# Which engine normalises the tokens of the third and fourth group in a Mamba-2 scan

## The reference, cut to what matters

```python
x = x + mamba2(_layernorm(x))          # the phase of this case
x = x + cross_attention(_layernorm(x), ctx, mask)
x = x + mixture_of_experts(_layernorm(x))

def _layernorm(x, axis=-1, eps=1e-05):
    m = jnp.mean(x, axis=axis, keepdims=True)
    v = jnp.var(x, axis=axis, keepdims=True)
    return (x - m) / jnp.sqrt(v + eps)

# mamba2, HID 256, 64 heads of 64 channels, state 128:
proj = hidden_states @ W_in.T          # z, xBC, dt
xBC = silu(conv4(xBC) + conv_b)        # x, B, C
dt = softplus(dt + dt_bias)
y = (C B^T * decay) @ (x * dt) + D_param * x      # over a sequence of 256
g = y * silu(z)
out = rmsnorm(g) * norm_w @ W_out.T
```

## Time and profile before

| | |
|---|---|
| median of three runs | 1668.36 us (1668.01 to 1669.1) |
| the profiled execution | 1666.68 us, of which the span from first to last instruction is 1664.9 us |
| mean granted TensorE clock | 0.989 of full speed |
| TensorE busy (matmul) | 1592.1 us, 96% |
| VectorE busy | 1250.4 us, 75% |
| ScalarE busy | 1198.9 us, 72% |
| GpSimd busy | 834.6 us, 50% |
| the 128 steps of the scan | from about 43 us to about 920 us |

### The profile page before, as it was taken

One profiled execution on the slowest core, in us unless ns is written; L12 is line 12 of the kernel. 1 busy time (PEld: TensorE's weight loads), 2 busy tenths in 40 slices (PEclk: granted clock), 3 DMA queues, 4 the chain that ended last, 5 costly groups with the idle time before them and its releaser, 6 DMA issues. The chain is left out here.

```text
span 1664.9 us, 29161 instructions
## 1 busy us (share of the span) xinstructions
PE 1592.1 (96%) x9876; PEld 1280.0 (77%) x9876; DVE 1250.4 (75%) x1954; ACT 1198.9 (72%) x2504; POOL 834.6 (50%) x677
## 2 busy tenths in 40 slices
PE   4998999999999999999999999999969999999999
PEld 3776777777777777777777667877748889999888
DVE  6899999999898999998899656766566534433355
ACT  5998899999999999999999566766624334444331
POOL 5798786565555555555565422211124563335460
PEclk8999999999999999999999999999979999999999
DMA  7555454444444454464542100000214323222231
GB/s 287 184 171 178 172 188 169 138 162 157 156 158 147 152 166 166 154 247 157 169 156 89 57 1 14 14 14 27 104 73 166 127 105 111 93 93 93 78 101 51
DMA packets 76238, 209.84 MB, mean 126 GB/s; under 512 B 9152, under 2 KB 32960, under 8 KB 74304
## 3 DMA queue, kind: packets, MB, share of 16 engines
q1 hardware_dynamic: 70432, 181.90, 32.0%
q0 software_dynamic: 5664, 26.09, 4.5%
HBM read 170.99 MB, written 36.96 MB: 125 GB/s over the span
## 5 line engine op out<-in xcount | busy, mean ns | idle before, releaser
L1011 PE MATMUL banks<-pair_hi,m_wxz 128*128 128x512 f32 x1024 | 352.3, 405 | 3.9 <-DVE pair_lo L664 2.3
L739 DVE SCALAR_TENSOR_TENSOR m_xc<-banks,m_cw,m_xc 128x510 f32<-128x510 f32 (+2 forms) x384 | 285.4, 743 | 11.0 <-ACT m_xc L502 1.3
L385 POOL TENSOR_TENSOR m_mat<-m_mat,m_cb_off 128x512 f32<-128x512 f32 x128 | 166.3, 1300 | 205.8 <-DVE m_mat L751 197.6
L516 ACT ACTIVATE m_mat<-m_a_all,m_cum 128x256 f32<-128x256 f32 x512 | 258.9, 506 | 1.6 <-PE m_ps_y L1052 1.6
L1068 PE MATMUL m_ps_out<-m_won,m_gT 128*128 128x256 f32 x1024 | 242.9, 380 | 4.7 <-POOL m_gT L394 3.2
L1011 PEld LDWEIGHTS banks<-pair_hi,m_wxz 128*128 128x128 f32 x1024 | 193.9, 189 | 42.8 <-issue 2.7
L394 POOL TENSOR_TENSOR m_gT<-m_gy,m_zs 128x512 f32<-128x512 f32 x128 | 167.0, 1305 | 107.2 <-DVE m_gy L781 106.9
L1068 PEld LDWEIGHTS m_ps_out<-m_won,m_gT 128*128 128x128 f32 x1024 | 191.4, 189 | 36.7 <-POOL m_gT L394 6.6
L519 ACT ACTIVATE m_mat<-m_a_all,m_cum 128x128 f32<-128x128 f32 x512 | 203.4, 397 | 0.0
L1011 PE MATMUL banks<-pair_lo,m_wxz 128*128 128x512 f32 x512 | 201.0, 393 | 0.0
L1052 PE MATMUL m_ps_y<-m_mat,m_xdt 128*64 128x256 f32 (+1 forms) x2048 | 194.7, 332 | 0.0
(11 more groups left out here) (348 smaller groups left out, 3400.4 us busy)
## 6 DMA issues: line engine op xcount, KB each, us to landing
m_a_all<-a_by_head SPq DMA_DIRECT2D x128, 512.0 KB, 4.0
m_wxz<-w_split SPq DMA_DIRECT2D x96, 512.0 KB, 5.0
w_split<-m_wxz SPq DMA_DIRECT2D x32, 512.0 KB, 3.0
raw<-in_w_gate_up POOLq DMA_DIRECT2D x9, 1280.0 KB, 6.8
raw<-in_w_xz SPq DMA_DIRECT2D x32, 256.0 KB, 3.9
raw<-in_w_down POOLq DMA_DIRECT2D x9, 640.0 KB, 7.8
x_sorted<-f_gT_hi SPq DMA_DIRECT2D x1, 4992.0 KB, 16.4
f_xg<-x_sorted SPq DMA_DIRECT2D x39, 128.0 KB, 2.6
```

The lines of the kernel that those rows point to most:

```text
L385: pool.tensor_tensor(off, off, cb_off[:, g * BG:(g + 1) * BG, :].rearrange("p b t -> p (b t)").unsqueeze(1) .broadcast_to([P, HPT, BG * P] ...
L516: act.activation(first_rows(u, h, b), a_all[u][:, h, b * SEQ:(b + 1) * SEQ].rearrange("p (j t) -> p j t", t=P), ACT.Relu, bias=cum[:, t, h ...
L739: dve.scalar_tensor_tensor(out=out[:, :, k:], in0=ps[:, :, 0:SEQ - k], scalar=cw[:, c, TAPS - 1 - k:TAPS - k], in1=out[:, :, k:], op0=ALU. ...
L1011: last = pe.matmul(ps[:, :], w, a, start=m == 0, stop=m == len(terms) - 1)
```

## The change

The eight normalisations of the tiles of the third and fourth group move from GpSimd to ScalarE. They are written as one activation with a bias and a scale for each partition: `x * rstd + (-mean * rstd)`. GpSimd forms the bias, `-mean * rstd`, for four tiles at once with two small operations in step 5, after `ln_root`. ScalarE does two tiles in step 10 and two in step 12, behind `tanh_z` and ahead of `decays` in its order. The new tile `off_mean` has 16 numbers a partition, and two semaphores, `ln_minus` and `ln_off`, are new. TensorE's, VectorE's and SyncE's programs are the same, and so is what is computed, up to rounding.

```diff
--- before.py
+++ after.py
@@ -120,6 +120,7 @@
         st = sb("st", [P, NT, 6])
         mv = sb("mv", [P, NT, 2])
         rstd = sb("rstd", [P, NT])
+        off_mean = sb("off_mean", [P, NT])
 
         wxz = [sb(f"wxz{u}", [P, 2, 2, KK, P], F32R)[:] for u in range(3)]
         a_all = [sb(f"a_all{u}", [P, HPT, TG])[:] for u in range(3)]
@@ -169,6 +170,7 @@
             sem(n) for n in ("consts_done", "fold_done", "ln_stats", "ln_aggr", "ln_veps", "ln_rstd"))
         small_hi, small_lo, won_act, won_pool = (
             sem(n) for n in ("small_hi", "small_lo", "won_act", "won_pool"))
+        ln_minus, ln_off = sem("ln_minus"), sem("ln_off")
         normed, normed_late, xT_ready, xT_hi_done, xT_lo_done = (
             sem(n) for n in ("normed", "normed_late", "xT_ready", "xT_hi_done", "xT_lo_done"))
         dtT_ready, dtT_done, dt_ready, dt_step, dt_exp, a_exp, a_neg, dA_done = (
@@ -343,11 +345,12 @@
                 pool.wait_ge(ln_veps, g + 1)
                 pool.tensor_tensor(rstd[:, ts], rstd[:, ts], neg_half[:, ts], ALU.pow).then_inc(ln_rstd, 1)
 
-            def normalise(n):
-                pool.wait_ge(ln_rstd, n // TPG + 1)
-                pool.wait_ge(xT_ready, n - TPG - (TPG if n < EARLY + TPG else 0) + 1)
-                pool.tensor_scalar(xn[:, xn_slot(n), :], xres[:, n, :], mv[:, n, 0:1], rstd[:, n:n + 1],
-                                   ALU.subtract, ALU.mult).then_inc(normed_late, 1)
+            def ln_offset(g):
+                ts = slice(g * TPG, (g + 1) * TPG)
+                pool.tensor_scalar(off_mean[:, ts], mv[:, ts, 0], -1.0, 0.0, ALU.mult, ALU.add).then_inc(ln_minus, 1)
+                pool.wait_ge(ln_rstd, g + 1)
+                pool.wait_ge(ln_minus, g - 1)
+                pool.tensor_tensor(off_mean[:, ts], off_mean[:, ts], rstd[:, ts], ALU.mult).then_inc(ln_off, 1)
 
             def small_low():
                 pool.wait_ge(small_hi, 2)
@@ -444,8 +447,7 @@
                 if g < NG - 2:
                     if j == 5:
                         ln_root(g + 2)
-                    if 7 <= j < 7 + TPG:
-                        normalise((g + 2) * TPG + j - 7)
+                        ln_offset(g + 2)
             root(NG - 1)
 
         @block.scalar
@@ -546,8 +548,17 @@
                 for k in range(KK):
                     act.activation(xT_hi[:, k, :], wq_raw[:, k, :], ACT.Copy).then_inc(wq_copied, 1)
 
+            def normalise(n):
+                act.wait_ge(ln_off, n // TPG - 1)
+                act.wait_ge(xT_ready, n - TPG - (TPG if n < EARLY + TPG else 0) + 1)
+                act.activation(xn[:, xn_slot(n), :], xres[:, n, :], ACT.Identity, bias=off_mean[:, n:n + 1],
+                               scale=rstd[:, n:n + 1]).then_inc(normed_late, 1)
+
             def prepare_next(n):
                 h, j = n // NCT + 1, n % NCT
+                if j in (10, 12) and h + 1 < NG:
+                    for n in range(2):
+                        normalise((h + 1) * TPG + n + (2 if j == 12 else 0))
                 if j == 3:
                     bc_scale(h, 0)
                 if j == 4:
```

## The result

The changed kernel takes 1671.4 us (median of 20 runs, 1669.57 to 1674.23) beside 1668.56 us for the kernel before in the same sessions (20 runs, 1666.12 to 1671.52). The ratio is 1.0017, with a 95% interval from 1.001 to 1.0024: 2.8 us slower. The forecast was 1668.1 us, practically no change, with a range up to 1670.8; the time lies 0.6 us above that range and on the other side of before. The profiled execution has a span of 1669.9 us, 5.0 more than that of before.

What follows compares the result with a forecast made beforehand. GpSimd and VectorE were taken to set the first group's pace, TensorE the second's. The terms -2.1 + 0.6 + 0 + 0 + 1.2 = -0.3 us gave 1668.1 us, range 1664.8 to 1670.8.

Steps and rivals of the forecast that it cites:

- Part 4: ScalarE gains two tiles in steps 10 and 12: first group 0, second group 1.2 us later, bounds 0 to 1.8.
- part 2: Two small operations join GpSimd in step 5: 0.6 us lost in the first group, free in the second.
- Part 1: Line 349 leaves GpSimd in the first group, steps 7 to 10: 2.1 us gained, bounds 1.1 to 4.1.
- my reference: First group's steps 15 to 18, without line 349, 7.59 us each, taken as the step length after the change.
- The rival with the lock: GpSimd and VectorE exclude each other at a shared port: three first-group tiles give back 3.6 us; 1666.6 us, chance 0.2.
- Part 3: Line 349 leaves GpSimd in the second group: worth 0 to 0.2 us, taken as 0.
- It does nothing: First group stays at 8.2 us a step, waiting behind line 405; only costs remain, +1.8, 1670.2 us, chance 0.14.
- ScalarE becomes the bound: ScalarE hands on its full pairs in both groups: +3.1 us, 1671.5 us, chance 0.08.
- the 0.2% that had a chance of 0.83: Whole kernel: a measurement tells 0.2%, 3.3 us, from no change; a result within that had chance 0.83.
- the stated bounds: Whole kernel: lower bounds of the costs with the upper bound of the gain, said to reach down to 1664.8 us.

Runs made afterwards that it cites:

- e1: The kernel before plus only the unused 64-byte tile off_mean, allocated ahead of the projection weights wxz: 1672.47 us, ratio 1.0032.
- e2: The whole change, with off_mean allocated behind all other buffers of the phase instead of ahead of wxz: 1667.17 us, ratio 0.9993 to before.
- e4: e2 with only the third group's tiles on ScalarE; the fourth group's stay on GpSimd: 1666.75 us, ratio 0.998 to before.
- e5: e2 with only the fourth group's tiles on ScalarE; the third group's stay on GpSimd: 1671.56 us, ratio 1.001 to before.
- e8: e4 with the two small bias operations in GpSimd's step 8 instead of step 5: 1667.75 us, ratio 0.9989 to before.
- e3: The kernel before plus an unused 64-byte tile just behind wxz, so wxz stays and all later buffers move: 1667.73 us, ratio 0.9999.
- e11: e5 with each normalised tile written twice by ScalarE, first into a spare buffer that nothing reads: 1672.84 us, ratio 1.0014 to before.

## Why the prediction was wrong, point by point

**The missing term.** Part 4 and part 2 were priced as instructions; the new buffer was priced nowhere, since a tile of 16 numbers looked free. It was the largest term: +4.5 us alone (e1), 0.05 us in each of the steps that TensorE paces. This is the step that failed: the prediction put the allocation at nothing without a reason, and by it the twelve projection matmuls take 2.89 us instead of 2.84. Where VectorE is the pace (steps 13 to 28) it costs little: +0.11 us in e1, +0.02 in the changed kernel. With the tile out of the way the same instructions are at -0.8 us (e2), and the forecast of -0.3 lies inside the interval, -2.7 to +0.2.

**Part 1, the relief in the first group, right in kind, too small.** Forecast -2.1, measured -3.1 (-3.07 in the changed kernel, -3.12 in e2). The mechanism is seen in the order of time. GpSimd and VectorE of one step after the change:

```profile
115.45 1.27 POOL L408 TENSOR_TENSOR m_g_sum<-m_g_sum,m_g_sq 128x512 f32<-128x512 f32 x1
118.48 1.27 POOL L388 TENSOR_TENSOR m_mat<-m_mat,m_cb_off 128x512 f32<-128x512 f32 x1 [1.76 <-DVE m_mat L762]
```

```profile
115.59 1.67 DVE L728 SCALAR_TENSOR_TENSOR raw<-xn_ffn,m_cw,raw 128x508 f32<-128x508 f32 x1
117.19 1.21 DVE L762 TENSOR_TENSOR m_mat<-m_mat,m_cb_diag 128x1024 f32<-128x1024 f32 x1
```

Beside the earlier trace rows: line 408 takes 1.27 us (1.74 before), line 762 takes 1.21 (2.29 before), GpSimd has 1.76 us idle ahead of line 388, and line 388 starts 0.08 us after 762 ends instead of 1.08. The tap, line 728, takes 1.67 us beside line 408; in the second group of the same kernel it takes 0.74. The step is 7.40 us, not the 7.59 of my reference: those reference steps carry two polynomial operations on VectorE that these don't (VectorE is busy 29.96 us of their 30.38 after the change, and 29.34 of the 29.62 here). I also counted from VectorE's second line 751, which left out the first tile; all four tiles gave back 0.77 to 0.93 us of a step. The rival with the lock asked for 3.6 us and was the nearer of the two.

**Part 2, the bias operations, right.** Forecast +0.6 in the first group, measured +0.67 in the changed kernel and +0.58 in e2 and e4; nothing in the second, where e2 and e5 also have them (TensorE's starts, under part 3). Their rows, beside the earlier trace rows:

```profile
94.04 1.85 POOL L346 TENSOR_TENSOR m_rstd<-m_rstd,logits 128x4 f32<-128x4 f32 x1
95.97 0.20 POOL L350 TENSOR_SCALAR m_off_mean<-m_mv 128x4 f32<-128x4 f32 x1
96.32 0.20 POOL L353 TENSOR_TENSOR m_off_mean<-m_off_mean,m_rstd 128x4 f32<-128x4 f32 x1
96.47 1.30 POOL L388 TENSOR_TENSOR m_mat<-m_mat,m_cb_off 128x512 f32<-128x512 f32 x1
```

e8 shows that this was a matter of the place: in step 8 the same two cost nothing.

**Part 3, nothing from line 349 in the second group, right.** The second group's four normalisations lie in steps 39 to 42. e4 keeps them on GpSimd, e2 and e5 don't, and up to step 44 TensorE's transposes start at the same times beside before in all three, to 0.01 us. VectorE's line 751 comes 0.24 us earlier in e2 and e5 in steps 41 and 42, and this is not handed on to TensorE.

**Part 4, ScalarE, right.** The price of a pair was 0.9 us from rows, and an estimated 0.98 by the Trainium skill, page "ScalarE: Activation LUTs", section "What ACT_TABLE_LOAD costs". The trace of after agrees with the page:

```profile
123.11 0.60 ACT L537 ACTIVATE banks<-m_xc 128x512 f32<-128x512 f32 x1 [0.48 <-DVE m_xc L750]
...
124.65 1.08 ACT L554 ACTIVATE xn_ffn<-xres,m_off_mean,m_rstd 128x256 f32<-128x256 f32 x2
125.63 1.47 ACT L527 ACTIVATE m_mat<-m_mat 128x1536 f32<-128x1536 f32 x1
...
130.51 0.60 ACT L537 ACTIVATE banks<-m_xc 128x512 f32<-128x512 f32 x1
```

124.65 to 125.63 is 0.98 us. In the first group it used up the idle time ahead of `tanh_x` (1.74 before, none here) and cost nothing that the trace shows: VectorE, the pace there, never waits for ScalarE between 100 and 150 us and is busy 49.54 of these 50 us both before and after, and e4 loses nothing behind step 13. No kernel takes line 349 off GpSimd without giving it to ScalarE, so the -3.1 us is the sum of both. In the second group the forecast was +1.2; e5 measured +1.17, e2 +1.18 between steps 40 and 48 (in the changed kernel +1.15, of which the same eight steps of e1 explain 0.44 by the layout; about +0.7 is left; that slower matmuls leave ScalarE more room would explain it, but wasn't tested). The path was the one forecast, seen in the waits of the changed kernel, VectorE for ScalarE and then TensorE for VectorE:

```profile
368.80 2.31 DVE L750 SCALAR_TENSOR_TENSOR m_xc<-banks,m_cw,m_xc 128x510 f32<-128x510 f32 x3 [0.63 <-ACT m_xc L504]
382.30 2.31 DVE L750 SCALAR_TENSOR_TENSOR m_xc<-banks,m_cw,m_xc 128x510 f32<-128x510 f32 x3 [0.30 <-ACT m_xc L504]
```

```profile
387.53 0.66 PE L1050 MATMUL banks<-ident,m_xs 128*128 128x128 f32 x4 [0.69 <-DVE m_xs L767]
```

In e2 the transposes fall behind before by 0.19, 0.17, 0.16 and 0.66 us in steps 45 to 48. TensorE's idle time between 340 and 400 us rises less than the forecast 1.2 us: from 0.43 us before to 1.35 in e2 and 0.99 in the changed kernel.

**The sum.** With the measured sizes the instructions give +0.6 - 3.1 + 1.2 = -1.3 us in e2's trace (-1.17 from step 0 to step 127, measured -0.8, interval -2.7 to +0.2). The layout adds 4.5 in e1. Together that is 3.7 by the medians of e2 and e1, where the changed kernel's show 2.8; by the traces from step 0 to step 127 it is -1.17 + 5.17 = 4.0, where the changed kernel has +3.22. The terms are not quite additive: about 0.5 us of the payback is missing with slower matmuls, and the rest is small against the intervals.

**The rivals.** All four were about instructions, so none could name the cause. "It does nothing" and "ScalarE becomes the bound" are refuted by e2's trace (3.12 us gained in the first group). The measured +0.17% lies within the 0.2% that had a chance of 0.83, but that was no merit of the mechanism, and the range ended 0.6 us too low, because it was built from known terms only. Its lower end doesn't follow from the stated bounds either: 4.1 us below before is 1664.3, not 1664.8.

## What to carry to other kernels

- Moving an elementwise instruction off GpSimd pays where VectorE and GpSimd make each other wait, here 0.8 us a step for a 1.2 us instruction, and paid nothing where TensorE was the pace. Move only those that meet that case (e4), and look at the receiving engine's idle time in each stage for itself.
- A new buffer is part of a change. Put it behind the others, as e2 does, or keep the distance between the two operands of the matmuls that set the pace; and if a stretch that the change doesn't touch gets slower at the same clock, try the allocation alone first.

## What was not expected of the hardware

- In this kernel the twelve 128x512 float32 matmuls of a step's projections take 2.84 us or 2.89, depending on the distance between their weights and their moving operand in SBUF: 64 bytes more 2.89, 128 bytes more 2.87, 256 or 512 bytes more 2.84. The output projection did not react: in e3 its operands `gT` and `won` also move apart by 64 bytes, and it stays at 1.89 us.
- Executions differ outside the scan, where the kernels hardly differ. Ahead of it the start of the first step differs by up to 1.8 us between traces (+0.17 in e1, +1.40 in after, +1.83 in e11, against before). From the last step's line 385 to the end of the span it is 1.3 us less than before in e1 and 4.0 us more in e11. 35 executions of before on one chip spread from 1664.0 to 1670.4 us of span as well. The traces also differ in TensorE's early matmuls, which stay slow for longer in after. Before, two 128x512 matmuls of the B and C projection:

```profile
17.27 0.55 PE L983 MATMUL m_ps_y<-pair_hi,m_wbc_lo 128*128 128x512 f32 x1
17.66 0.40 PE L983 MATMUL m_ps_y<-pair_hi,m_wbc_hi 128*128 128x512 f32 x1
```

 and after:

```profile
17.31 0.63 PE L994 MATMUL m_ps_y<-pair_hi,m_wbc_lo 128*128 128x512 f32 x1
17.74 0.63 PE L994 MATMUL m_ps_y<-pair_hi,m_wbc_hi 128*128 128x512 f32 x1
```

 The same instruction takes 0.40 us before and 0.63 after. The granted clock reads 1.00 from 17 to 19 us in both traces, so it doesn't show a lower clock as the cause, and the cause stays open. For a change of this size a single pair of spans (5.0 us apart here) says little; the difference by step says where.
